# First loop of a two-layer decoder: inputs loaded with channels on partitions, and the linear attention's state cut into 32-column tiles

## The reference, cut to what matters

```
q, k, v = x@Wq + bq, x@Wk + bk, x@Wv + bv        # each (512, 8 heads, 32)
Q, K = elu(q) + 1, elu(k) + 1
KV  = einsum('nshd,nshv->nhdv', K, v / 512)      # one 32x32 state per head
Z   = 1 / (einsum('nlhd,nhd->nlh', Q, K.sum(axis=1)) + 1e-6)
out = einsum('nlhd,nhdv,nlh->nlhv', Q, KV, Z) * 512
x   = layernorm(x + out)
x   = layernorm(x + cross_attention(x, ctx))     # 16 heads, 64 context tokens
```

## Time and profile before

| | us |
|---|---|
| runs (3): median, lowest, highest | 1372.87, 1371.81, 1374.49 |
| span of the profiled execution | 1374.7 |
| TensorE busy in it | 1243.7 (90%) |
| VectorE busy | 1048.2 (76%) |
| ScalarE busy | 517.7 (38%) |

### The profile page before, as it was taken

How to read it: one execution, slowest core, us unless ns; L and a number is a source line. 1 busy time by engine, 2 the same in 40 slices (tenths; PEclk the granted TensorE clock), 3 DMA queues, 4 the chain that set the end, 5 groups by cost and what they waited for, 6 DMA issues and landing times.

```text
span 1374.7 us, 18473 instructions
## 1 busy us (share of the span) xinstructions
PE 1243.7 (90%) x7340; PEld 828.6 (60%) x7340; DVE 1048.2 (76%) x1966; ACT 517.7 (38%) x608; POOL 267.8 (19%) x194
## 2 busy tenths in 40 slices
PE   7899999997999999853779999999999999998976
PEld 4566666665644554321566776767768686766654
DVE  3578899986634789998564787969878797887777
ACT  1244334433534567587013323232322333231421
POOL 0011111112100000033100413204132141413242
PEclk9899999999999999976899999999999999999998
DMA  5001000102582045489322011100211000000000
GB/s 219 16 16 32 31 1 31 32 16 93 150 295 77 31 153 185 167 315 373 107 87 84 31 54 62 54 31 32 63 54 54 32 24 21 27 20 36 1 16 16
DMA packets 47829, 107.86 MB, mean 78 GB/s; under 512 B 10752, under 2 KB 31360, under 8 KB 44288
## 3 DMA queue, kind: packets, MB, share of 16 engines
q1 hardware_dynamic: 43584, 104.59, 21.7%
q10 hardware_dynamic: 4160, 2.10, 0.5%
HBM read 62.64 MB, written 44.04 MB: 78 GB/s over the span
## 4 chain that ended last, share of the span: by engine, by line
PE 74%; DVE 16%; DMA 3%; ACT 3%; issue 2%; POOL 1%; SPq 0%; POOLq 0%; ACTq 0%; DVEq 0%
PE ps L1357 8%; PE ps L1420 7%; PE ps L1236 6%; PE ps L1067 6%; PE ps L1118 4%; PE ps L817 4%; PE ps L1393 3%; PE ps L1302 3%; PE ps L965 2%; PE ps L890 2%; PE ps L1326 2%; PE ps L1337 2%; PE ps L1467 2%; DMA arena<-up_scratch 2%; PE ps L908 2%
## 5 line engine op out<-in xcount | busy, mean ns | idle before, releaser
L1420 PE MATMUL ps<-arena 128*128 128x256 f32 x512 | 120.1, 389 | 5.8 <-ACT arena L1892 5.8
L1357 PE MATMUL ps<-arena 128*128 128x512 f32 x256 | 117.6, 598 | 0.0
L1420 PEld LDWEIGHTS ps<-arena 128*128 128x128 f32 x512 | 98.6, 195 | 27.9 <-ACT arena L1892 9.9
L2535 DVE TENSOR_TENSOR arena<-ps,arena 128x2048 f32<-128x2048 f32 x32 | 73.3, 2292 | 38.1 <-PE ps L1302 37.9
L1938 POOL TENSOR_TENSOR arena<-arena 128x4 f32<-128x4 f32 x44 | 45.5, 1038 | 282.0 <-DVE arena L2124 282.0
L1998 POOL TENSOR_TENSOR arena<-arena 128x16 f32<-128x16 f32 x32 | 92.2, 2916 | 32.5 <-DVE arena L2564 32.5
L1236 PE MATMUL ps<-arena 128*128 128x256 f32 x384 | 88.2, 386 | 5.2 <-DVE arena L2456 5.2
L1067 PE MATMUL ps<-arena 128*128 128x512 f32 x192 | 83.8, 593 | 1.2 <-ACT arena L1620 1.2
L1118 PE MATMUL ps<-arena 128*128 128x512 f32 x192 | 84.4, 594 | 0.0
L1236 PEld LDWEIGHTS ps<-arena 128*128 128x128 f32 x384 | 73.0, 194 | 16.5 <-issue 7.0
L1357 PEld LDWEIGHTS ps<-arena 128*128 128x128 f32 x256 | 46.2, 190 | 48.7 <-issue 45.1
(11 more groups left out here) (311 smaller groups left out, 2651.9 us busy)
## 6 DMA issues: line engine op xcount, KB each, us to landing
v_scratch<-arena SPq DMA_DIRECT2D x7, 1536.0 KB, 12.9
arena<-v_scratch SPq DMA_DIRECT2D x7, 1536.0 KB, 6.8
up_scratch<-arena SPq DMA_DIRECT2D x6, 1536.0 KB, 6.0
arena<-up_scratch SPq DMA_DIRECT2D x6, 1536.0 KB, 12.6
vw_scratch<-arena SPq DMA_DIRECT2D x32, 256.0 KB, 3.8
arena<-x_scratch SPq DMA_DIRECT2D x16, 512.0 KB, 4.7
arena<-vw_scratch SPq DMA_DIRECT2D x8, 1024.0 KB
arena<-x SPq DMA_DIRECT2D x8, 512.0 KB, 5.7
```

Source lines behind the costliest of these rows:

```text
L1357: last = mm(flat(p % 2), w["cos_wq"][:, k, p * P:(p + 1) * P], xt4[:, k], start=k == 0, stop=k == NC - 1)
L1420: last = mm(flat(2)[:, C:2 * C], cos_pt[:, p], cos_vw[:, par, p], start=p == 0, stop=p == NP - 1)
L2535: v.tensor_tensor(met_s[:, n % 2].rearrange("p r t h n -> p (r t h) n"), flat(3, 4).rearrange("p (h n) -> p h n", n=P), w["causal"].unsque ...
```

## The change

The host hands in x a second time, already turned (`x_turned`: channels on partitions), and the context only turned. SP loads `x_turned` of a batch straight into `lin_xt` and, right behind it, x as before for the residual. `lin_turn_x`, `lin_copy_x`, the context's transposes and copy, and the scratch copy of the context are gone; the two later loads of the turned context read the input instead. The q, k and v projections wait for the DMA into `lin_xt`. `lin_state` computes each head's 32 by 33 block on its own, in the column tile of its 32 PSUM partitions; for this `lin_z` is laid out as (k or v, token tile, head, 32+1), and the mask spreads a block over the four head positions while it multiplies, for both channel halves in one operation.

```diff
-PACK_CTX = [("ctx", (B * TC // P, C))]
+PACK_CTX = [("ctx_t", (NC, B * TC))]
-        lin_z = ar.take(NT, 2 * C + 2)
+        lin_z = ar.take(2, NT, C // LD, LD + 1)
...
             def load_x(b, par):
                 if b.reg is None and b.off == 2:
                     sp.dma_start(ffn_all, pack_ffn).then_inc(loaded["pack_ffn"], 16)
-                    sp.wait_ge(ev("ctx_t_ready"), 1)
-                    sp.dma_start(ctx_d, ctx_t.rearrange("p a b c -> p (a b c)")).then_inc(ev("ctx_stored"), 16)
                 wait_back(sp, "y1_ready", b, 2)
+                sp.dma_start(lin_xt[:, par].rearrange("p a b -> p (a b)"), at_batch(x_turned, b))\
+                    .then_inc(moved("lin_xt_loaded", par), 16)
                 sp.dma_start(lin_x[:, par], at_batch(x_rows, b)).then_inc(moved("x_loaded", par), 16)
...
             pe.wait_ge(loaded["pack_ctx"], 16)
-            for c in range(NC):
-                for t in range(NT):
-                    last = tr(bank(c)[:, 0, t * P:(t + 1) * P], w["ctx"][:, t, c * P:(c + 1) * P], ident)
-            last.then_inc(ev("ctx_transposed"), 1)
-            pe.wait_ge(ev("ctx_t_ready"), 1)
             pe.wait_ge(loaded["pack_xat"], 16)
...
-            def lin_turn_x(b, par):
...
             def lin_project_q(c):
                 def step(b, par):
-                    wait(pe, "lin_x_copied", b)
+                    wait_moved(pe, "lin_xt_loaded", b, par)
...
             def lin_state(b, par):
                 for c in range(NC):
-                    at = C + c * (P + 1)
                     for t in range(NT):
-                        last = mm(flat(2)[:, c * (P + 1):(c + 1) * (P + 1)], lin_k[:, t, c * P:(c + 1) * P],
-                                  lin_z[:, t, at:at + P + 1], start=t == 0, stop=t == NT - 1)
+                        for g in range(4):
+                            h = 4 * c + g
+                            last = mm(flat(2)[LD * g:LD * g + LD, c * (LD + 1):(c + 1) * (LD + 1)],
+                                      lin_k[:, t, h * LD:h * LD + LD], lin_z[:, 1, t, h],
+                                      start=t == 0, stop=t == NT - 1, skip_group_check=True)
...
-                v.tensor_scalar(lin_ek, lin_z[:, :, 0:C], 0.0, None, ALU.min)\
+                v.tensor_scalar(by_head(lin_ek), lin_zk, 0.0, None, ALU.min)\
...
             def lin_mask_state(b, par):
-                for c in range(NC):
-                    lo, total = ((1, 0), (P + 1, 2 * P + 1))[c]
-                    v.tensor_tensor(lin_kv[:, c, 0:P], flat(2)[:, lo:lo + P], w["blk32"], ALU.mult)
-                    last = v.tensor_scalar(lin_kv[:, c, P:], w["blk32"][:, 0:P:LD], flat(2)[:, total:total + 1],
-                                           None, ALU.mult)
+                n = P // LD
+                states = flat(2)[:, 0:NC * (LD + 1)].rearrange("p (c n) -> p c n", c=NC)
+                v.tensor_tensor(lin_kv[:, :, 0:P].rearrange("p c (g n) -> p c g n", g=n),
+                                states[:, :, 0:LD].unsqueeze(2).broadcast_to([P, NC, n, LD]), ...)
+                last = v.tensor_tensor(lin_kv[:, :, P:], states[:, :, LD:].broadcast_to([P, NC, n]), ...)
```

More of the change, by code:

```diff
@@ L172, in width, with decoder @@
     return sum(int(np.prod(d)) for _, d in pack)
-def decoder(nc, x_in, pack_ident, pack_lin, pack_ctx, pack_xat, pack_ffn, pack_l1, pack_prep,
+def decoder(nc, x_in, x_turned, pack_ident, pack_lin, pack_ctx, pack_xat, pack_ffn, pack_l1, pack_prep,
             pack_wv, pack_wk, out):
@@ L543, in _ @@
         def _(sp):
-            for sbuf, dram, name in ((ctx_all, pack_ctx, "pack_ctx"), (ident_all, pack_ident, "pack_ident"),
+            for sbuf, dram, name in ((ctx_t.rearrange("p a b c -> p (a b c)"), pack_ctx, "pack_ctx"), (ident_all, pack_ident, "pack_ident"),
                                      (xat_all, pack_xat, "pack_xat"), (lin_all, pack_lin, "pack_lin")):
@@ L804, in step @@
                 def step(b, par):
-                    wait(pe, "lin_x_copied", b)
+                    wait_moved(pe, "lin_xt_loaded", b, par)
                     if t == 0:
-                        wait(pe, "lin_x_copied", b)
+                        wait_behind(pe, "xat_spread_copied", b, 3, 1, 1)
                         wait_behind(pe, "lin_scaled", b, 1, 1, 4)
                     if t == 1:
-                        wait(pe, "lin_x_copied", b)
                         wait_behind(pe, "lin_scaled", b, 1, 3, 4)
@@ L1513, in _ @@
             act.wait_ge(loaded["pack_lin"], 16)
[L1516 to L1519, removed]
             def lin_bias_q(b, par):
@@ L2064, in _ @@
             link = line.link
-            dve.wait_ge(ev("ctx_t_ready"), 1)
+            dve.wait_ge(loaded["pack_ctx"], 16)
             for c in range(NC):
@@ L2141, in lin_q_features @@
                                        op1=ALU.add).then_inc(sig("lin_q_ready").sem, 1)
-            def key_value(row):
-                return row.rearrange("p (a n) -> p a n", a=2)[:, :, 0:C]
             def lin_bias_kv(t):
@@ L2150, in step, with by_head @@
                     if b.first():
[L2151 to L2154, removed]
+                        v.memset(lin_z[:, 1, t, :, LD:], 1.0)
+                    v.tensor_tensor(lin_z[:, :, t, :, 0:LD], flat(t % 2).rearrange("p (a h d) -> p a h d", a=2, d=LD),
+                                    w["lin_bkv"].rearrange("p (a h d) -> p a h d", a=2, d=LD), ALU.add)\
                         .then_inc(sig("lin_kv_biased", NT).sem, 1)
                 return step
+            def by_head(rows):
+                return rows.rearrange("p t (h d) -> p (t h) d", d=LD)
+            lin_zk = lin_z[:, 0].rearrange("p t h d -> p (t h) d")[:, :, 0:LD]
             def lin_k_negative(b, par):
                 wait(dve, "lin_kv_biased", b, NT, NT)
-                v.tensor_scalar(lin_ek, lin_z[:, :, 0:C], 0.0, None, ALU.min)\
+                v.tensor_scalar(by_head(lin_ek), lin_zk, 0.0, None, ALU.min)\
                     .then_inc(sig("lin_k_negative").sem, 1)
@@ L2169, in lin_mask_state @@
                 wait(dve, "lin_state_done", b)
-                for c in range(NC):
-                    lo, total = ((1, 0), (P + 1, 2 * P + 1))[c]
-                    v.tensor_tensor(lin_kv[:, c, 0:P], flat(2)[:, lo:lo + P], w["blk32"], ALU.mult)
-                    last = v.tensor_scalar(lin_kv[:, c, P:], w["blk32"][:, 0:P:LD], flat(2)[:, total:total + 1],
-                                           None, ALU.mult)
+                n = P // LD
+                states = flat(2)[:, 0:NC * (LD + 1)].rearrange("p (c n) -> p c n", c=NC)
+                v.tensor_tensor(lin_kv[:, :, 0:P].rearrange("p c (g n) -> p c g n", g=n),
+                                states[:, :, 0:LD].unsqueeze(2).broadcast_to([P, NC, n, LD]),
+                                w["blk32"].rearrange("p (g n) -> p g n", g=n).unsqueeze(1).broadcast_to([P, NC, n, LD]),
+                                ALU.mult)
+                last = v.tensor_tensor(lin_kv[:, :, P:], states[:, :, LD:].broadcast_to([P, NC, n]),
+                                       w["blk32"][:, 0:P:LD].unsqueeze(1).broadcast_to([P, NC, n]), ALU.mult)
                 last.then_inc(sig("lin_kv_ready").sem, 1)
@@ L2812 @@
         "blk32": f32(p[:, None] // LD == p // LD),
-        "ctx": rows(a["ctx_1024"].reshape(B * TC, C)),
+        "ctx_t": rows(a["ctx_1024"].reshape(B * TC, C).T),
         "xat_wk": rows(a["L0_xattn_Wk"].T), "xat_bk": per_channel(a["L0_xattn_bk"]),
@@ L2839 @@
     }
-    arrays = {"x": np.ascontiguousarray(a["x"])}
+    turned = a["x"].reshape(B, T, NC, P).transpose(0, 3, 2, 1).reshape(B, P, NC * T)
+    arrays = {"x": np.ascontiguousarray(a["x"]), "x_turned": np.ascontiguousarray(turned)}
     for name, pack in PACKS.items():
```

27 lines of the change are left out of this document (5 added, 22 removed).

## The result

Seven runs of the changed kernel have a median of 1366.72 us (1365.32 to 1370.18); seven runs of the kernel before, on the same chip, one of 1374.25 us (1371.81 to 1379.98). The ratio is 0.9946 [0.9931, 0.9962]: 7.4 us faster, with an interval of 5.2 to 9.5. Against the 1372.87 us that stood ahead of the forecast it is 6.2 us. Two executions of the kernel before beside the later experiments, of 1404 and 1519 us at a mean granted clock of 0.92 and 0.83 (0.96 to 0.97 in all others), are in a slower state and left out of every comparison.

A forecast was written before the change was run, and what follows sets the result against it. Two equal chains, on TensorE and VectorE, were taken to bound full turns, so gains come only where the pipeline fills: -1.5 - 2.3 - 1.2 - 1.0 = -6.0 us, from 1372.87 to 1366.9 us; 8-in-10 range 1362.5 to 1371.5.

The forecast's parts named there:

- What bounds a full turn: Output projection to fourth scores: equal TensorE and VectorE chains meet within 0.1 us; idle time there becomes 1.5 to 2 us.
- Turn 8 of before: Turn without transposes of x: 9.56 us from output projection to fourth scores against turn 7's 9.57, with 1.05 us idle.
- A, the context: Program start: key projection needs only its loads and starts at about 6.2 us; -1.5 us (-2.5 to -0.5).
- B, the first transposes: Program start: L817 follows the value projection at once, without the first transposes of x and ScalarE's copy; -2.3 us.
- C, the state in turn 1: Turn 1's state of 3.81 us shrinks to 2.6 us at half clock; -1.2 us (-2.6 to 0).
- the bound of -2.6: Turn 1's state: the largest gain in term C's range of -2.6 to 0 us.
- the lower bound of 0.6: State at full clock: 0.6 us if time scales with columns from L926's 2.2 us; upper bound 1.89, taken 1.3.
- D, turn 2: Turn 2: third scores move up until they meet VectorE's shift, shorter state included; -1.0 us (-1.85 to -0.5).
- E, full turns: Turns 3 to 8: no gain, 0.0 us, by the equality of turns 7 and 8.
- F, VectorE's edits: VectorE's two-operation mask and the minimum over k at a stride of 33 words: nothing (0 to +1.1 us).
- The clock rival: Longer idle before fourth scores drops the clock, 1.69 us a fall; three falls give 1370.3 us, six 1375.3; chance 0.22.
- The waiting tiles: State passes wait for the previous pass in their tile: state 4.7 us, total +13.8 us, 1386.7 us; chance 0.08.

The follow-up runs named there:

- the reordered pair of kernels: VectorE's second shift moved before q's features, its statistics and maximum moved later: on the changed kernel 1356.88 us (ratio 0.9887), on the kernel before 1372.13 us (0.9987).
- its first edit alone: Changed kernel with VectorE's second shift ahead of q's features and its statistics behind the third shift and mask: 1364.92 us, ratio to before 0.9936.

## Why the forecast held, and which terms were off

The forecast's median, 1366.9 us, was met within 0.2 us, and that much is luck. It started from the 1372.87 us of three runs; the seven runs give 1374.25, 1.4 us more, and the gain was 7.4 us instead of 6.0. The terms one by one:

**What bounds a full turn** was read rightly: two equal chains, and what TensorE gives up becomes idle time. Turn 8 of before, used as the test, was a good one; the transposes put back, and the reordered pair of kernels, show both chains by themselves. The idle time is 2.18 us and not 1.5 to 2, because the state is shorter than I took it: 1.05 + 1.89 - 0.70 = 2.24.

**A, the context** (-1.5): key projection at 6.38 for 6.2 forecast, released by the load, and 5.91 instead of 6.00 us long, so nothing was taken back there. With the value projection's end it came to -1.37. It is not the same each time: in the eight profiles with the new start the key projection took 5.23 to 6.54 us, in the three with the old one 6.00 to 6.45. The forecast put its length down to the half clock, which the profiles do not show: the granted clock reads 1.00 from 7.6 to 13.5 us before and from 6.4 to 12.0 after, though the passes take 1061 ns in the median and 592 at the least. What slows them stays open.

**B, the first transposes** (-2.3): -2.30 (3.67 less 1.37). No wait of TensorE for the loads of x turned shows in the loop.

**C, the state in turn 1** (-1.2): this term was mis-sized. From the state's start to the output's it is 1.54 us after and 4.67 before, -3.13, and so more than the bound of -2.6. Two things were off. The state is 0.70 us, near the lower bound of 0.6 that went by columns, where I took twice that. And in this profile it ran at the full clock, where I had set the half one. The size counts for more: in the second profile the clock was at 0.50 there, and from the state's start to the output's (35.62) it is still only 1.73 us, -2.94:

```profile
33.89 1.11 PE L807 MATMUL ps<-arena 128*32 128x33 f32 x64 [3.87 <-DVE arena L2135]
```

Granted clock (the column behind the engines' busy times) of TensorE around it, in turn 4 and behind the fourth scores of turn 7:

```profile
33.30:34.60 1.30, 0.77 (x64) 0.65 (x64) 1.30 (x3) 0.00 (x0) 0.00 (x0) 1.00 0.00 0
36.00:38.00 2.00, 2.00 (x11) 2.00 (x11) 1.63 (x7) 0.00 (x0) 0.00 (x0) 0.50 0.00 0
39.00:46.00 7.00, 7.00 (x17) 3.06 (x17) 4.26 (x16) 0.52 (x1) 3.38 (x2) 1.00 0.00 1
133.60:136.90 3.30, 3.30 (x8) 2.63 (x9) 3.27 (x3) 0.00 (x0) 0.00 (x0) 0.53 0.00 0
261.40:264.80 3.40, 3.40 (x29) 3.03 (x30) 3.00 (x11) 0.98 (x1) 0.00 (x0) 1.00 0.00 0
```

At 36 to 38 us the clock is half, and from 39 us on it is whole again, where before it was half throughout 37 to 46. The shorter stretch gave another 0.66 us until the first scores of turn 2 (-7.55 there, -6.89 at the output), a term that I did not have. In the second profile of the changed kernel the start and turn 1 together were 0.9 us slower, so this part of the gain is not the same in each execution. Nor is what it is measured against: with the old state turn 1 took 22.77, 22.69, 21.86 and 20.64 us in four profiles of four kernels, and with the tiled one, its tiles in turn, 19.28 to 19.82 in six. The half clock behind the state lasted some 10 us in the only trace of the kernel before and some 3 in that of the same kernel with VectorE's two edits. So the 3.4 us that turn 1 gained are the upper end; against the shortest of the four it would be about 1.

The Trainium skill, TensorEngine Tiling (Array Packing), section Instruction Overhead, has about 60 cycles for each product on trn2; for 64 passes that made 1.6 us as an estimate, and counted by the 32 products it would be 0.8. The trace differs: 64 passes of 33 columns stepped in 0.70 us at a granted clock of 1.00, less than half of the one and less than the other. The measurement decides.

**D, turn 2** (-1.0): -0.74 from the second scores to the fourth (8.76 to 8.02 us) in the first profile, and -0.02 (8.74 us) in the second, where the half clock behind the second scores lasted 6.7 us; so the term is not sure. Each part alone got none of it: with the tiled state alone the transposes of probabilities waited for ScalarE, with the loads alone the half clock lasted as long as in the second profile.

**E, full turns** (0): turns 3, 6 and 7 within 0.02 us. Turn 4 cost 0.39 us more: VectorE waited 2.42 us for the output projection, 2.04 before, though both projections took 5.41 us. It recurs in other kernels with the tiled state (41.20 and 41.08 us) and not with the loads alone (40.70); why is not settled.

**F, VectorE's edits** (0): the minimum over k at the new stride, as a group:

```profile
L2130 DVE TENSOR_SCALAR arena<-arena 128x1024 f32<-128x1024 f32 x8 | 5.6, 696 | 0.3
```

696 ns against 695. By the Trainium skill's rule on even outermost dimensions (VectorE: DVE Perf Modes, section on the mode 2x_2P) it was to stay; the trace agrees.

Summed in the first profiles: -1.37 - 2.30 - 0.09 (an earlier release of the state) - 3.13 - 0.66 - 0.02 (first to second scores) - 0.74 + 0.39 - 0.01 = -7.93 at the last mark, where the forecast had -6.0. The second profile of the changed kernel has -6.48.

**The clock rival** did not come: behind the fourth scores' idle time of 2.18 to 2.56 us the clock was whole in all twelve turns of the two profiles (the last of the rows above is turn 7's). The same idle time in front of the second scores of turn 4 was followed by half clock in both kernels (132.42 and the row of 133.60 above; the earlier trace rows). But the place does not decide either: with VectorE's order changed twice, 2.55 us there kept the clock in turns 4 and 5, and with its first edit alone 2.18 us kept it in turn 4 (the output projection behind took 3.72 us) and not in turn 5 (5.41 us). What tells the cases apart is not settled; TensorE is busy without a gap for over 7 us ahead of both places. That no fall came behind the fourth scores is therefore measured, and not explained. **The waiting tiles** fell with 0.70 us, and with the 1.46 us of the state tile by tile.

## What to carry to other kernels

Where two engines' chains run side by side and meet, look for a turn of the trace that lacks one of them: it tells what taking that work away is worth. If nothing, the gain is latent: move the other engine's work that nobody waits for (here statistics and a maximum) behind the step that is waited for, and both edits pay together, here another 8 to 10 us (3.4 of them the clock's in turns 4 and 5, in the one profile there is), where each alone left turns 3, 6 and 7 as they were. Look then at what the moved work now stands in front of; the first of the two edits lost, in turns 6 and 7, two thirds of its gain (37.23 instead of 36.37 us a turn) to a new wait.

## What was not expected of the hardware

Float32 products of 33 columns step at 11 ns a pass when four column tiles take turns and at 23 ns when the four products of a sum follow each other in one tile (granted clock 1.00). And the clock's half stretches move by several microseconds between kernels and between executions of one kernel, with the same work before them: the changed kernel's turn 2 took 31.73 us in one profile and 32.50 in the next. A change of a few microseconds is therefore better read from marks in the time line, turn by turn, than from the total, and from more than one trace of either kernel; here the kernel before had only one.
